# Experts' second layer: an fp32 product is written as products of fp32r halves

## The reference, cut to what matters

```python
xb = jnp.einsum('nec,nd->ecd', sec_mask, xf)                 # 8 experts, 1280 slots each, 192 wide
h = jax.nn.gelu(jnp.einsum('ecd,edf->ecf', xb, fc_w) + fc_b) # first layer, 192 -> 768
out = jnp.einsum('ecf,efd->ecd', h, pj_w) + pj_b             # second layer, 768 -> 192
y = jnp.einsum('nec,ecd->nd', cb_weight, out)
```

## Time and profile before

| what | value |
|---|---|
| runs | 1266.61 us median, 1260.33 to 1267.8 (3 runs) |
| the profiled execution, its own time | 1269.29 us |
| its span, first to last instruction | 1267.1 us |
| experts, first matmul to the end of the span | 924.0 to 1267.1 us |
| one expert, in the middle | 41.6 to 41.7 us |

### The profile page before, as it was taken

One profiled execution on the slowest core, in us unless ns is written; L12 is line 12 of the kernel. 1 busy time (PEld: TensorE's weight loads), 2 busy tenths in 40 slices (PEclk: granted clock), 3 DMA queues, 4 the chain that ended last, 5 costly groups with the idle time before them and its releaser, 6 DMA issues.

```text
span 1267.1 us, 22341 instructions
## 1 busy us (share of the span) xinstructions
PE 1050.1 (83%) x7466; PEld 777.2 (61%) x7466; DVE 724.3 (57%) x2995; ACT 601.8 (47%) x1169; POOL 628.2 (50%) x702
## 2 busy tenths in 40 slices
PE   2597968879698788888888888884589999999997
PEld 1455645555465555656556556541478888988896
DVE  4566769587686565767567566645533433433431
ACT  1136757566587885443443444331544344434432
POOL 7745556453533335445345444521236766576654
PEclk9967989889899898979979989975589999999999
DMA  6110000000000000010110110112445444564342
GB/s 136 47 34 16 23 21 26 9 26 19 16 1 2 1 2 2 1 30 2 30 30 2 30 31 1 30 31 38 107 74 84 96 84 94 76 104 77 72 54 30
DMA packets 49165, 50.38 MB, mean 40 GB/s; under 512 B 14437, under 2 KB 42408, under 8 KB 49064
## 3 DMA queue, kind: packets, MB, share of 16 engines
q0 software_dynamic: 19456, 26.84, 13.6%
q1 hardware_dynamic: 29610, 22.30, 6.7%
HBM read 33.87 MB, written 15.24 MB: 39 GB/s over the span
## 4 chain that ended last, share of the span: by engine, by line
PE 66%; DVE 16%; issue 6%; ACT 6%; POOL 0%; POOLq 0%; ACTq 0%; DVEq 0%
PE ps_ring L678 12%; PE ps_scores L678 11%; PE ps_ring L670 11%; PE ps_ring L905 9%; PE ps_scores L790 5%; PE ps_ctx L807 4%; PE ps_scores L905 4%; DVE xn L1291 4%; PE ps_scores L793 2%; DVE probs L1252 2%; PE ps_ring L747 2%; DVE probs L1258 1%; PE ps_ring L746 1%; PE ps_ring L737 1%; DVE xin L1214 1%
## 5 line engine op out<-in xcount | busy, mean ns | idle before, releaser
L545 POOL DMA_INDIRECT out<-z_t,slots_now x80 | 129.6, 1620 | 115.4 <-DVE z_t L1531 94.2
L1103 ACT ACTIVATE probs<-ps_scores,fc_bias 128x512 f32<-128x512 f32 (+1 forms) x144 | 88.3, 616 | 162.8 <-PE ps_scores L678 154.9
L1006 ACT ACTIVATE prob_t<-ps_ring 128x512 f32<-128x512 f32 x192 | 115.1, 600 | 94.7 <-PE ps_ring L670 91.4
L530 POOL TENSOR_TENSOR probs<-probs,neg_max 128x512 f32<-128x512 f32 x96 | 100.9, 1051 | 118.5 <-DVE neg_max L1258 118.4
L670 PE MATMUL ps_ring<-ident,probs 128*128 128x128 f32 x768 | 133.1, 301 | 19.6 <-DVE x_hi L1170 6.6
L1252 DVE CUSTOM_DVE_ANT_0 probs<-square 128x128 f32<-128x128 f32 x384 | 111.7, 344 | 53.7 <-ACT square L1015 47.2
L678 PE MATMUL ps_ring<-x_hi,w_hi 128*128 128x512 f32 x240 | 111.2, 463 | 22.2 <-ACT k L974 10.4
L1258 DVE CUSTOM_DVE_ANT_0 probs<-ps_scores,causal 128x128 f32<-128x128 f32 x384 | 88.7, 285 | 67.9 <-PE ps_scores L793 66.4
L670 PEld LDWEIGHTS ps_ring<-ident,probs 128*128 128x128 f32 x768 | 97.0, 153 | 47.9 <-issue 15.6
L905 PE MATMUL ps_ring<-work,probs 128*128 128x192 f32 x672 | 117.1, 328 | 7.0 <-issue 4.4
L530 POOL TENSOR_TENSOR probs<-probs,row_root 128x512 f32<-128x512 f32 x96 | 99.4, 1054 | 45.2 <-ACT probs L1024 44.8
(11 more groups left out here) (214 smaller groups left out, 2358.0 us busy)
## 6 DMA issues: line engine op xcount, KB each, us to landing
work<-pj_w SPq DMA_DIRECT2D x8, 576.0 KB
token_in<-xin SPq DMA_DIRECT2D x8, 384.0 KB, 3.3
out<-resid SPq DMA_DIRECT2D x8, 384.0 KB, 4.3
vals<-fc_w SPq DMA_DIRECT2D x8, 384.0 KB
vals<-fc_w SPq DMA_DIRECT2D x16, 192.0 KB
out<-z_t,slots_now POOLq DMA_INDIRECT x80
token_in<-xin SPq DMA_DIRECT2D x8, 128.0 KB, 4.3
got<-pj_b SPq DMA_DIRECT2D x8, 96.0 KB
```

Of the source, the lines that this page charges most:

```text
L530: gp.tensor_tensor(probs[:, j, :, :], probs[:, j, :, :], shift.unsqueeze(2).to_broadcast([128, 4, 128]), ALU.subtract).then_inc(p.shifted, 1)
L545: gp.indirect_dma_start(out[:, :], bass.IndirectOffsetOnAxis(slots_now[:, u, 1, t:t + 1], 0), slot_y[:, o, :], None, compute_op=ALU.add).t ...
L1006: sc.activation(prob_t[:, s % 2, :, :], src.rearrange("p (h q) -> p h q", h=4), ACT.Exp, scale=1.0 if p is mag else -1.0).then_inc(ring_fr ...
L1103: sc.activation(hidden[:, c % 2, f_, 0:128 * nt], ps_scores[:, i, 0:128 * nt], ACT.Gelu, bias=fc_bias[:, e, f_:f_ + 1]).then_inc(gelu_done ...
```

## The change

The second layer's fp32 product is replaced by products of fp32r halves. The weights are split once an expert: ACT writes the high half into columns 0 to 191 of `pj_parts` (`second_weights_high`; the tensor lies in `w_hi` or `w_lo` of the attention), DVE the low half beside it into columns 192 to 383 (`split_second`). The activations are split for each group of features: ACT evaluates the GELU a second time, into the fp32r tensor `hidden_hi`, and DVE subtracts it from `hidden` into `hidden_lo` (`split_hidden`). PE then runs, for each of the 6 groups of a tile, one matmul with the high activations against the 384 columns of high and low weights, and one with the low activations against the 192 columns of high weights, added to the first half of the bank. DVE adds the second half of the bank to the first (`y_summed`). In the first tile of a chunk PE waits group by group for `hidden_split`, where it waited for all GELUs of the chunk. The tensors of the attention are laid out so that the new ones can lie over them; ACT and DVE wait once for the stores that read these.

```diff
--- before.py
+++ after.py
@@ -158,8 +158,18 @@
         ps_ring = pb("ps_ring", [128, RING, 512])
 
 
-        resid = sb("resid", [128, SEQS, HID])
-        xin = sb("xin", [128, SEQS, HID])
+        with ExitStack() as attention_only:
+            early = lambda name, shape: attention_only.enter_context(nc.sbuf_tensor(name, shape, F32))
+            resid = early("resid", [128, SEQS, HID])
+            xin = early("xin", [128, SEQS, HID])
+            q_of = [early(f"q{u}", [128, BLOCKS, GROUP, 128]) for u in range(2)]
+            k_of = [early(f"k{u}", [128, BLOCKS, GROUP, 2, 128]) for u in range(2)]
+        hidden_hi = sb("hidden_hi", [128, 2, FF_CHUNKS, 512], F32R)
+        hidden_lo = sb("hidden_lo", [128, 2, FF_CHUNKS, 512], F32R)
+        low_hot_at = sb("low_hot", [128, BLOCKS * GROUP * 128], F32R)
+        high_hot_at = sb("high_hot", [128, BLOCKS * GROUP * 128], F32R)
+        fc_hi = sb("fc_hi", [128, 2, 2, FF], F32R)
+        fc_lo = sb("fc_lo", [128, 2, 2, FF], F32R)
         logits = sb("logits", [128, SEQS, EXPERTS])
         ident = sb("ident", [128, 128])
         causal = sb("causal", [128, 128])
@@ -200,14 +210,6 @@
         got_pos = got[:, GROUP * HID:2 * GROUP * HID].rearrange("p (s d) -> p s d", s=GROUP)
         got_dom = got[:, 2 * GROUP * HID:].rearrange("p (s d) -> p s d", s=GROUP)
 
-        with ExitStack() as attention_only:
-            early = lambda name, shape: attention_only.enter_context(nc.sbuf_tensor(name, shape, F32))
-            q_of = [early(f"q{u}", [128, BLOCKS, GROUP, 128]) for u in range(2)]
-            k_of = [early(f"k{u}", [128, BLOCKS, GROUP, 2, 128]) for u in range(2)]
-        low_hot_at = sb("low_hot", [128, BLOCKS * GROUP * 128], F32R)
-        high_hot_at = sb("high_hot", [128, BLOCKS * GROUP * 128], F32R)
-        fc_hi = sb("fc_hi", [128, 2, 2, FF], F32R)
-        fc_lo = sb("fc_lo", [128, 2, 2, FF], F32R)
         vals_of = [vals[:, :, :, :], work[:, 2560:4096].rearrange("p (s h d) -> p s h d", s=GROUP, h=HEADS)]
         stats = sb("stats", [128, GROUP, 6])
         moments = sb("moments", [128, GROUP, 2])
@@ -304,6 +306,7 @@
 
         raw_fc = vals[:, :, :, :].rearrange("p s h d -> p (s h d)").rearrange("p (c n) -> p c n", c=2)
         pj_w_sb = work[:, 2 * FF:2 * FF + 2 * FF_CHUNKS * HID].rearrange("p (u c n) -> p u c n", u=2, c=FF_CHUNKS)
+        pj_parts = [w[:, :, :, :].rearrange("p c m n -> p (c m) n") for w in (w_hi, w_lo)]
         pj_bias = got[:, 0:EXPERTS * HID].rearrange("p (e n) -> p e n", e=EXPERTS)
 
         ROW = 256 + TOPK
@@ -351,6 +354,11 @@
         fc_high = sem("fc_high")
         pj_loaded = [sem(f"pj_loaded{u}") for u in range(2)]
         pj_used = [sem(f"pj_used{u}") for u in range(2)]
+        pj_high = sem("pj_high")
+        pj_split = sem("pj_split")
+        hidden_split = sem("hidden_split")
+        y_summed = sem("y_summed")
+        pj_ready = lambda n, v: (pj_loaded[v], n * 8 + 16 - 8 * v)
         x_loaded = [sem(f"x_loaded{c}") for c in range(3)]
         ex_turn_full = [sem(f"ex_turn_full{i}") for i in range(2)]
         ex_turn_free = [sem(f"ex_turn_free{i}") for i in range(2)]
@@ -893,17 +901,19 @@
             def second_layer(r, u, e, c):
                 t0, nt = CHUNKS[c]
                 if c == 0:
-                    pe.wait_ge(pj_loaded[u], 16 * r + 16)
-                for i in range(FC_RING):
-
-                    pe.wait_ge(gelu_done[i], e * 6 + 2 * c + 3)
+                    pe.wait_ge(pj_split, e + 1)
                 for t in range(t0, t0 + nt):
                     i, n = y_place(e, t)
                     pe.wait_ge(y_free[i], n + 1)
                     tok = slice(128 * (t - t0), 128 * (t - t0) + 128)
                     for f_ in range(FF_CHUNKS):
-                        last = pe.matmul(ps_y[i][:, 0:HID], hidden[:, c % 2, f_, tok], pj_w_sb[:, u, f_, :],
-                                         start=(f_ == 0), stop=(f_ == FF_CHUNKS - 1))
+                        if t == t0:
+
+                            pe.wait_ge(hidden_split, e * (len(CHUNKS) * FF_CHUNKS) + FF_CHUNKS * c + f_ + 1)
+                        pe.matmul(ps_y[i][:, 0:2 * HID], hidden_hi[:, c % 2, f_, tok], pj_parts[u][:, f_, :],
+                                  start=(f_ == 0), stop=False, skip_group_check=True)
+                        last = pe.matmul(ps_y[i][:, 0:HID], hidden_lo[:, c % 2, f_, tok], pj_parts[u][:, f_, 0:HID],
+                                         start=False, stop=(f_ == FF_CHUNKS - 1), skip_group_check=True)
                     last.then_inc(y_full[i], 1)
 
             def expert(r, u, more):
@@ -1076,6 +1086,13 @@
                 apart(act)
                 sc.activation(fc_hi[:, u, :, :], raw_fc, ACT.Copy).then_inc(fc_high, 1)
 
+            def second_weights_high(n, v):
+
+                loaded, count = pj_ready(n, v)
+                act.wait_ge(loaded, count)
+                apart(act)
+                sc.activation(pj_parts[v][:, :, 0:HID], pj_w_sb[:, v, :, :], ACT.Copy).then_inc(pj_high, 1)
+
             def whole_x(e, c):
                 t0, nt = CHUNKS[c]
                 for m in range(t0 // 2, (t0 + nt) // 2):
@@ -1101,6 +1118,8 @@
                     act.wait_ge(fc_full[i], e * 6 + 2 * c + f_ // FC_RING + 1)
                     apart(act)
                     sc.activation(hidden[:, c % 2, f_, 0:128 * nt], ps_scores[:, i, 0:128 * nt], ACT.Gelu,
+                                  bias=fc_bias[:, e, f_:f_ + 1])
+                    sc.activation(hidden_hi[:, c % 2, f_, 0:128 * nt], ps_scores[:, i, 0:128 * nt], ACT.Gelu,
                                   bias=fc_bias[:, e, f_:f_ + 1]).then_inc(gelu_done[i], 1)
 
             def expert(e, u, more):
@@ -1111,13 +1130,18 @@
                     expert_weights_high(e + 1, 1 - u)
                 gelus(e, 1)
                 whole_x(e, 2)
+                if more:
+                    second_weights_high(e + 1, 1 - u)
                 gelus(e, 2)
                 if more:
                     whole_x(e + 1, 0)
 
             act.wait_ge(bias_loaded, 16 * (1 + EXPERTS))
             expert_weights_high(0, 0)
+            second_weights_high(0, 0)
             whole_x(0, 0)
+
+            act.wait_ge(resid_stored, 16 * GROUPS)
             with act.Fori(0, EXPERTS // 2 - 1, 1) as r:
                 expert(r * 2, 0, True)
                 expert(r * 2 + 1, 1, True)
@@ -1487,6 +1511,20 @@
                     ve.tensor_tensor(fc_lo[:, u, :, :], raw_fc, f(fc_hi[:, u, :, :]), ALU.subtract
                                      ).then_inc(raw_split, 1)
 
+                def split_second(n, v):
+                    loaded, count = pj_ready(n, v)
+                    dve.wait_ge(loaded, count)
+                    dve.wait_ge(pj_high, n + 1)
+                    ve.tensor_tensor(pj_parts[v][:, :, HID:2 * HID], pj_w_sb[:, v, :, :],
+                                     f(pj_parts[v][:, :, 0:HID]), ALU.subtract).then_inc(pj_split, 1)
+
+                def split_hidden(e, c):
+                    for f_ in range(FF_CHUNKS):
+                        dve.wait_ge(gelu_done[f_ % FC_RING], e * 6 + 2 * c + f_ // FC_RING + 2)
+                        tok = slice(0, 128 * CHUNKS[c][1])
+                        ve.tensor_tensor(hidden_lo[:, c % 2, f_, tok], hidden[:, c % 2, f_, tok],
+                                         f(hidden_hi[:, c % 2, f_, tok]), ALU.subtract).then_inc(hidden_split, 1)
+
                 def take_weights(e, u, c):
 
                     t0, nt = CHUNKS[c]
@@ -1525,6 +1563,10 @@
                         if not (isinstance(e, int) and e == 0 and t < OUT_RING):
                             dve.wait_ge(y_stored[o], e * (16 * CAP_TILES // OUT_RING) + 16 * (t // OUT_RING))
                         ve.tensor_tensor(slot_y[:, o, :], ps_y[i][:, 0:HID], pj_bias[:, e, :], ALU.add
+                                         ).then_inc(y_summed, 1)
+                        dve.wait_ge(y_summed, e * CAP_TILES + t + 1)
+                        apart(dve)
+                        ve.tensor_tensor(slot_y[:, o, :], ps_y[i][:, HID:2 * HID], slot_y[:, o, :], ALU.add
                                          ).then_inc(y_free[i], 1)
                         dve.wait_ge(y_free[i], n + 2)
                         dve.wait_ge(slot_w_made, len(CHUNKS) * e + c + 1)
@@ -1532,18 +1574,25 @@
                                          ALU.mult).then_inc(y_scaled[o], 1)
 
                 def expert(e, u, more):
+                    split_hidden(e, 0)
                     split_x(e, u, 1)
                     add_bias(e, u, 0)
                     if more:
                         split_weights(e + 1, 1 - u)
+                    split_hidden(e, 1)
                     split_x(e, u, 2)
                     add_bias(e, u, 1)
                     if more:
+                        split_second(e + 1, 1 - u)
+                    split_hidden(e, 2)
+                    if more:
                         split_x(e + 1, 1 - u, 0)
                     add_bias(e, u, 2)
 
```

(2 more changed lines are left out.)

## The result

| | before | after |
|---|---|---|
| median of 8 runs | 1265.54 us (1259.6 to 1267.8) | 1274.64 us (1269.63 to 1281.35) |
| ratio | | 1.0087, 95% interval 1.0065 to 1.0110 |
| the profiled execution | 1269.29, span 1267.1 | 1281.35, span 1278.1 |
| first matmul of the experts to the span's end | 924.03 to 1267.1: 343.1 | 927.84 to 1278.1: 350.3 |

The change makes the kernel 0.9% slower; 1278 had been forecast. Of the 11.0 us between the two spans the experts hold 7.2. The other 3.8 lie before them, in code that the change does not touch: over all profiles of this study the first expert begins anywhere from 913.7 to 927.8.

What follows compares the result with a forecast made beforehand. PE was taken to bound the experts. Seven handovers (+6.7), three table loads (+3.1) and the last expert (-0.4) sum to +9.4 us on 1269.29, so 1278.7, forecast as 1278; range 1266 to above 1297.

Steps and rivals of the forecast that it cites:

- Both stalls: PE idle about 1.6 us before chunk 0's fourth tile (DVE's second add) and 2.1 at each handover (DVE's last x half).
- The pair: PE's second layer: one 384-column plus one 192-column matmul per product, 0.287 us, ends 0.228 and 0.345; a tile 1.72.
- the third rival: PE's second layer: cheap 384-column matmuls make the kernel not slower, 1267 us, deciding below a pair of 0.24; chance 0.12.
- The second rival: First layers: ACT becomes the bound; a GELU step of 0.614 gives 1286 us, no overlap 28 more; chance 0.12.
- the main sum: All experts, full clock: gains and waits of the chunks, handovers and table loads add +9.4 us; chance 0.50.
- Chunk 0: First four-tile chunk of an expert: PE waits for the fourth tile's bank, 16.8 us against 16.3, +0.5.
- Chunk 1: Second four-tile chunk of an expert: one x pair to make, no stall, 15.1 us against 16.1, -1.0.
- the 9.95 in front of them: Time from a four-tile chunk's first matmul to the end of its first second-layer tile: 9.95 us.
- Chunk 2: Last chunk of an expert: the chain through ACT and DVE ends at 10.75 us against 9.30, +1.45.
- The first expert's chunk 0: Chunk behind a table load: last GELU 1.2 us later, 0.15 of it paid before, on top of the usual +0.5.
- The other two table loads: Two of three experts starting a round of ACT's loop: last GELU 1.2 us later, 0.15 paid before; all three +3.1.
- The clock: Handovers: PE's clock falls behind the 2.1 us gap, 1.7 lost each, seven times 12, 1290 us; chance 0.22.

Runs made afterwards that it cites:

- e5: Changed kernel with a second x_full buffer, so ACT writes the second pair while DVE splits the first; ratio to the kernel before 0.9886.
- e2: Changed kernel with one GELU a group, the low half of the activations left out (zero); ratio to the kernel before 0.9945, 1260.76 us.
- e8: Changed kernel run again unchanged beside the others on another chip, with a second profile; ratio to the kernel before 1.0054.
- e10: Changed kernel with a second x_full buffer, and POOL's four gathers behind chunk 0's stores started later; ratio to the kernel before 0.9944.
- e11: Changed kernel without the 192-column matmul of low activations with high weights, 480 matmuls less; ratio to the kernel before 1.0054.
- e3: Changed kernel without DVE's second add; the product with the low weights is computed but left out of the output; ratio to the kernel before 1.0117.
- e4: Changed kernel with the row weights computed behind the adds instead of in front of the x pairs; ratio to the kernel before 1.0101.
- e6: Changed kernel with both a second x_full buffer and the row weights behind the adds; ratio to the kernel before 0.9915.
- e7: Kernel before with a second x_full buffer and the row weights behind the adds, second layer still fp32; ratio to the kernel before 0.9945.

## Why the prediction was right, and where not

**The mechanism held.** Both stalls came where they were put, with the releasers that were named: 1.3 to 1.5 for 1.6 before the fourth tile, 2.1 to 2.3 for 2.1 at the handover. PE's busy time over the whole of the experts went from 323.8 to 310.4 us, 13.4 less for the 18 forecast; the two falls of the clock hide about 3 of it. e5 shows the stalls are the cause: with nothing changed but a buffer, the sign turns.

**The pair** was forecast at 0.287 with ends 0.228 and 0.345 and is 0.286, the tile 1.72. So the third rival, not slower by a cheap pair, is out, and by its own condition. The Trainium skill (TensorE: Matmul & The Clock Gate, section Back-to-back issue gap) gives N / 2.4 + 2.5 ns as the gap of an isolated matmul; the pair would have been 0.245 by it, an estimate. The trace does not agree for this data type in a dense row.

**ACT** kept up: a step of 0.571 to 0.583 where the clock was up, and no wait of PE for it in a 4-tile chunk but two of 0.4 behind a table load. The second rival is out; what e2 took away is ACT's part in the two chains, which the main sum had. The 0.614 estimated from the Trainium skill (ScalarE: Activation LUTs, section What ACT_TABLE_LOAD costs) was too much by these rows.

**The terms.** Chunk 0 +0.4 to +0.5 for +0.5: right. Chunk 1 was -1.25 for -1.0: the three tiles of 1.72 were right, and what was mis-sized is the 9.95 in front of them, by 0.25: the last low half ends at 9.3 for 9.4, and PE, which waits for it, follows faster than the 0.14 + 0.1 that I gave it. Chunk 2 was +1.2 for +1.45, each step of its chain 0.1 to 0.25 early from the first GELU on (0.92 behind the first matmul for 1.02). The first expert's chunk 0, forecast at +1.55, gained nothing: 18.83 before and 18.84 after. PE begins it at a low clock in both kernels (1.2 GHz up to 929 and 931), so by my reading it took as long before as the chain through ACT and DVE takes after, and I had priced it from a chunk at full clock. The other two table loads cost 1.2 each (17.9 for 16.7), of which 0.13 was paid before, so 1.05 was right. In all 9.4 becomes about 4.4.

**The clock**, put in a rival at 1.7 us for each of seven handovers, belongs into the sum at a fraction: two falls of 1.4 in this execution (4.4 + 2.8 = 7.2, the measured difference of the experts), five in e8. The row that spoke against it, 2.08 us in the attentions with no fall, was a single case, and a single case of a thing that happens sometimes says little. So the main sum was about 5 too high and the clock, left out of it, is missing with about 3 to 6. The medians differ by 9.1, which is as good as the 9.4 of the sum, but partly by luck, because these two cancel. Where the 9.1 has what it has over the 7.2 of the experts, two profiled executions do not tell.

## What to carry to other kernels

When a change takes work from the bounding engine and gives it to two that stand behind it, write out the chain from their last operation to the buffer that the first one wants next, and look for a wait in that chain that a buffer removes, before judging the change: here 1.09 us of waiting for `x_full`, twice an expert, decided between 1.005 and 0.989 on one chip, with the falls of the clock that go with it. Keep idle times of TensorE short in dense work even where they look paid for; in the experts of these runs the clock never fell behind one of up to 1.65 us, it fell behind about half of those from 1.67 to 2.9 (26 of 49), and behind all seven of 3.2 and more. A fall cost 1.3 to 1.5 us in a chunk of four tiles, 0.4 where PE waited for ACT anyway. And measure what is done to the old kernel by the same repairs, since it may want them too.

## What the runs showed of the hardware

- The granted clock fell to 1.2 GHz behind a wait of 2.09 us and not behind one of 2.08, in one execution of one kernel. Over all profiles the shortest wait with a fall behind it was 1.69 (e10), the longest without one 2.86 (e11). How often differs between executions (two of seven handovers, then five).
- In five kernels (e2, e3, e4, e6, and once in e7) some chunks had PE's results reach DVE or ACT 0.6 to 2.3 us later than its matmuls are on record, at full granted clock. None in the sixteen experts of after's two profiles, nor in e5; six of eight in e4. No run told the cause.
- In a pair the 192-column matmul is followed after 0.09 by the next, where in a row of its own kind it takes 0.111, and the 384-column one takes 0.20 where its columns alone would be 0.176. The sum is the same to 0.001; the single terms are not.
- The median of a kernel whose PE has less to do (e11) need not move at all: 480 matmuls less, about 53 us by the 0.111 of the earlier trace rows, bought nothing.
